# Image attention of a Flamingo kernel: scores per head pair, once with queries and once with keys on the partitions

## The reference

```python
l = layer_norm(layernorm(x), ln2_g, ln2_b)          # 4 batches x 512 rows x 128
c = layer_norm(ctx_1024, ln1_g, ln1_b)              # 4 x 154 x 128
q = l @ Wq                                          # 16 heads of 64
k, v = split(concat([c, l], axis=1) @ Wkv, 2)       # 666 keys and values a batch
w = softmax((q * 64 ** -0.25) @ (k * 64 ** -0.25).T)   # 512 x 666 for each batch and head
x = x + tanh(g_xattn[0]) * (w @ v) @ Wo
```

## Time and profile before

| | us |
|---|---|
| median of 3 runs | 2148.45 (2147.19 to 2157.12) |
| profiled execution, whole | 2145.17 |
| its span, first to last instruction | 2143.4 |
| busy in the span: PE, DVE, ACT, POOL | 1784.1, 1257.3, 969.9, 216.6 |
| image attention, first projection (L588) to last update of x (L710) | 17.8 to 795.6 |

### The profile page before, as it was taken

The page is one execution under the profiler, slowest core; times in us unless marked ns, Lnnn a source line. Parts: engine busy times, 40 slices in busy tenths (PEclk is TensorE's granted clock), DMA queues, the critical chain, the costliest instruction groups (busy, mean ns, idle before and its releaser), DMA issues.

```text
span 2143.4 us, 31509 instructions
## 1 busy us (share of the span) xinstructions
PE 1784.1 (83%) x11792; PEld 1060.9 (49%) x11792; DVE 1257.3 (59%) x2971; ACT 969.9 (45%) x2067; POOL 216.6 (10%) x263
## 2 busy tenths in 40 slices
PE   4899999999999987998615878995985886579997
PEld 2465655665665556776404544552443333324444
DVE  4766566656656644776496665655457455644333
ACT  3677667756756744996101624554211442201111
POOL 1100111111100000000000233300001301200000
PEclk9999999999999997999655879997997687779998
DMA  6000000000000010001000000000000000000000
GB/s 240 10 18 14 20 14 14 20 14 14 20 14 14 14 47 1 2 2 75 0 0 0 1 8 5 1 2 1 1 1 1 1 1 0 1 0 1 6 5 10
DMA packets 14584, 32.83 MB, mean 15 GB/s; under 512 B 3593, under 2 KB 9057, under 8 KB 13537
## 3 DMA queue, kind: packets, MB, share of 16 engines
q1 hardware_dynamic: 14433, 30.81, 4.6%
HBM read 18.84 MB, written 1.05 MB: 9 GB/s over the span
## 4 chain that ended last, share of the span: by engine, by line
PE 68%; DVE 22%; ACT 5%; issue 4%; POOL 2%; DMA 0%; ACTq 0%; DVEq 0%; POOLq 0%
PE banks L449 12%; PE banks L642 7%; PE banks L629 7%; PE banks L618 5%; PE banks L1589 3%; PE banks L2205 3%; PE banks L2201 3%; DVE work L668 3%; DVE xn L395 2%; DVE work L720 2%; PE banks L1572 2%; PE banks L573 1%; PE banks L2253 1%; PE banks L424 1%; PE banks L1498 1%
## 5 line engine op out<-in xcount | busy, mean ns | idle before, releaser
L749 ACT ACTIVATE work<-banks,work 128x666 f32<-128x666 f32 x256 | 209.1, 817 | 235.0 <-DVE work L668 205.5
L668 DVE TENSOR_REDUCE work<-banks 128x1 f32<-128x666 f32 x256 | 217.0, 848 | 84.8 <-PE banks L618 76.3
L642 PE MATMUL banks<-work 128*64 128x256 f32 (+1 forms) x1536 | 221.4, 395 | 13.8 <-ACT work L764 12.7
L629 PE MATMUL banks<-const,work 128*128 128x128 f32 (+1 forms) x1536 | 220.6, 280 | 6.3 <-ACT work L764 5.9
L449 PE MATMUL banks<-work,weights_b 128*128 128x512 bf16 x864 | 201.0, 389 | 13.1 <-DVE work L1913 5.2
L629 PEld LDWEIGHTS banks<-const,work 128*128 128x128 f32 (+1 forms) x1536 | 154.9, 134 | 80.3 <-issue 70.9
L618 PE MATMUL banks<-work 128*128 128x512 bf16 (+1 forms) x1024 | 188.3, 306 | 3.6 <-issue 3.6
L686 DVE COPY work<-banks 128x256 f32<-128x256 f32 x256 | 107.8, 421 | 84.8 <-PE banks L629 81.7
L618 PEld LDWEIGHTS banks<-work 128*128 128x128 bf16 x1024 | 97.9, 98 | 111.5 <-issue 41.6
L764 ACT ACTIVATE work<-banks 128x512 f32<-128x512 f32 x256 | 151.0, 590 | 2.1 <-PE banks L629 2.0
L424 PE MATMUL banks<-const,xn 128*128 128x128 f32 x176 | 39.3, 364 | 131.7 <-DVE xn L395 80.7
(11 more groups left out here) (344 smaller groups left out, 3130.2 us busy)
## 6 DMA issues: line engine op xcount, KB each, us to landing
work<-work SPq DMA_DIRECT2D x64, 166.5 KB, 2.7
weights_b<-in_weights SPq DMA_DIRECT2D x1, 4116.0 KB, 23.2
weights_b<-in_weights SPq DMA_DIRECT2D x1, 2824.0 KB, 9.3
weights_a<-in_weights SPq DMA_DIRECT2D x1, 2056.0 KB, 8.5
weights_a<-in_weights SPq DMA_DIRECT2D x1, 2050.0 KB, 9.5
rows<-in_rows SPq DMA_DIRECT2D x1, 1496.0 KB, 12.6
weights_c<-in_weights SPq DMA_DIRECT2D x1, 1288.0 KB, 26.3
weights_b<-in_weights SPq DMA_DIRECT2D x1, 1027.5 KB, 12.7
```

The costliest lines, as they stand in the source:

```text
L629: m = pe.transpose(ps[0:rows, c:c + P], prob[:, t * P:t * P + rows], self.eye)
L642: m = pe.matmul(self.out_bank[64 * h:64 * h + 64, 0:2 * P], self.v[n % 3][0:rows, t, 64 * h:64 * h + 64], self.probs_t[u % 2][0:rows, h, t ...
L668: ve.tensor_reduce(self.neg_max[i % 4], self.slot[i % 2][:, 0:KEYS0], AX_X, ALU.max, negate=True).then_inc(self.mark("max"))
L749: ac.activation(self.probs[i % 4], self.slot[i % 2][:, 0:KEYS0], ACT.Exp, bias=self.neg_max[i % 4], accum_out=self.sums[u % 2][:, 2 * j + ...
```

## The change

One image attention is replaced by another; the rest of the kernel stays. The work goes by pairs of heads n = 0 to 31. Scores are now made twice:

- with queries on the partitions, for the maxima alone (item "score", four a pair, both heads each): high half of q against bf16 keys, then the cross terms with the low halves. For the 512 image keys these are two matmuls that use 64 rows of the array each (L689, L690). VectorE takes both maxima ("max");
- with keys on the partitions (item "term", six a pair, the last with 26 keys): high part (L621), cross terms on 64 rows for each head (L624), and minus the maximum, which is turned by matmul ("lifted", L605), copied by ScalarE ("shifted") and added with ones over 32 rows for each head (L627). ScalarE then takes the exponential ("exp") straight into the operand of the values (L645; L643 for the 26). No probabilities are transposed, and none are copied.

The sums over keys are added by GpSimd over the terms ("sum"), and over the partitions by a matmul with ones ("total", L651); VectorE inverts 128 x 512 of them ("invert") and multiplies ("mix"). The two DMAs a pair now copy the high half of q. What is issued when is a table of times in pairs: a pair's projections are made during the pair before, its maxima in its own slot, its terms in the next, its total in the one after. All engines walk the sorted table.

```diff
-    def image_scores_pe(self, pe, i):
-        for a, z in ((0, SEQ), (SEQ, KEYS0)):
-            for part in (0, 1):
-                m = pe.matmul(slot[:, a:z], lhs, k[:, h, part, a:z], start=part == 0, stop=part == 1)
...
-    def image_turn_pe(self, pe, i):
-                m = pe.transpose(ps[0:rows, c:c + P], prob[:, t * P:t * P + rows], self.eye)
...
+    def image_items(self):
+
+        out = []
+        for n in range(GROUPS0):
+            first = n - 1 if n else -0.9
+            for at, what in ((0.02, "q"), (0.05, "q_high"), (0.14, "q_low"), (0.30, "k"), (0.33, "k_high"), (0.45, "k_low"),
+                             (0.60, "kc"), (0.63, "kc_high"), (0.76, "kc_low"), (0.78, "v"), (0.82, "v_keep")):
+                out.append((first + at, what, n, 0))
+            for i in range(QT):
+                out += [(n + 0.1 + 0.25 * i, "score", n, i), (n + 0.11 + 0.25 * i, "max", n, i)]
+            out += [(n + 0.98, "negate", n, 0), (n + 1.12, "lifted", n, 0), (n + 1.13, "shifted", n, 0)]
+            at = lambda i: n + 1.2 + 0.075 * i
+            for t in range(KT0):
+                out += [(at(2 * t), "term", n, t), (at(2 * t) + 0.001, "exp", n, t), (at(2 * t) + 0.002, "sum", n, t)]
+                out.append((at(2 * t + 3 if t < KT0 - 1 else 2 * t + 2), "weigh", n, t))
+            out.append((n + 2.17, "keep", n, 0))
+            out.append((n + 2.28, "total", n, 0))
+            out += [(n + 2.33 + 0.12 * j, "invert", n, j) for j in (0, 1)]
+            out += [(n + 2.36 + 0.12 * j, "mix", n, j) for j in (0, 1)]
+        for b in range(BATCH):
+            late = PAIRS * b + PAIRS + 1
+            for t, at in enumerate((0.8, 1.17, 1.8, 2.17)):
+                out += [(late + at, "bring", b, t), (late + at + 0.08, "add", b, t)]
...
+            elif what == "lifted":
+                bank = self.bank(pe, 7, "shifted", n)
+                if n == 0:
+                    pe.wait_ge(*self.at("dma_const_b", 16))
+                pe.wait_ge(*self.at("negated", n))
+                for t in range(QT):
+                    m = pe.matmul(bank[0:96, t * P:(t + 1) * P], self.neg_parts[n % 2][:, t, :], self.cb["eye_b"], start=True, stop=True)
+                m.then_inc(self.mark("lifted", n))
+            elif what == "term":
+                q_low, k, shifts = self.q_low[n % 3], self.k[n % 3], self.shifts[n % 2]
+                if i == 0:
+                    pe.wait_ge(*self.at("shifted", n))
+                    pe.wait_ge(*self.at("kc_low", n, 1))
+                rest = i == KT0 - 1
+                keys = slice(i * P, i * P + (WIDE if rest else P))
+                if rest:
+                    self.bank(pe, 3, "exp", n, i, 0)
+                    out = [self.bank_of(3)[0:WIDE, :], self.bank_of(3)[WIDE:2 * WIDE, :]]
+                else:
+                    out = [self.bank(pe, 3 + h, "exp", n, i, h) for h in (0, 1)]
+                width = WIDE if rest else P
+                for h in (0, 1):
+                    pe.matmul(out[h], k[:, h, keys], self.q_high[n % 3][:, h, :], start=True, stop=False)
+                for h in (0, 1):
+                    half = slice(D0 * h, D0 * (h + 1))
+                    pe.matmul(out[h], k[half, h, keys], q_low[half, :], start=False, stop=False)
+                for h in (0, 1):
+                    rows = slice(D0 * h, D0 * h + WIDE)
+                    m = pe.matmul(out[h], ones[rows, 0:width], shifts[rows, :], start=False, stop=True)
+                    if not rest:
+                        m.then_inc(self.mark("term", n, i, h))
+                if rest:
+                    m.then_inc(self.mark("term", n, i, 0))
+            elif what == "weigh":
+                if i == 0:
+                    self.bank(pe, 5, "out_kept", n)
+                    pe.wait_ge(*self.at("v_kept", n))
+                    pe.wait_ge(*self.at("vc_kept", n))
+                rest = i == KT0 - 1
+                pe.wait_ge(*self.at("exp", n, i, 0 if rest else 1))
+                for h in (0, 1):
+                    out = self.bank_of(5)[D0 * h:D0 * (h + 1), :]
+                    if rest:
+                        rows = slice(WIDE * h, WIDE * h + CTX_REST)
+                        m = pe.matmul(out, self.v_rest[n % 3][rows, :], self.image_prob(n, i, 0)[rows, :], start=False, stop=True)
+                    else:
+                        m = pe.matmul(out, self.v[n % 3][:, i, D0 * h:D0 * (h + 1)], self.image_prob(n, i, h), start=i == 0, stop=False)
+                m.then_inc(self.mark("weighed", n, i))
+            elif what == "total":
+                bank = self.bank(pe, 6, "inverted", n, 1)
+                pe.wait_ge(*self.at("summed", n, KT0 - 1))
+                for h in (0, 1):
+                    m = pe.matmul(bank[D0 * h:D0 * (h + 1), :], self.c["ones_f"], self.sums[n % 2][h], start=True, stop=True)
+                m.then_inc(self.mark("total", n))
...
+    def image_scores_pe(self, pe, n, i):
+
+        q_high, q_low, k = self.q_high[n % 3], self.q_low[n % 3], self.k[n % 3]
+        cols = slice(i * P, (i + 1) * P)
+        if i == 0:
+            for h in (0, 1):
+                pe.wait_ge(*self.at(f"dma_query{n % 2}{h}", 16 * (n // 2 + 1)))
+            pe.wait_ge(*self.at("q_low", n, 1))
+            pe.wait_ge(*self.at("kc_low", n, 1))
+            pe.wait_ge(*self.at("vc_kept", n))
+        main, rest = slice(0, SEQ), slice(SEQ, KEYS0)
+        first = self.bank(pe, 0, "max", n, i, 0)
+        pe.matmul(first, q_high[:, 0, cols], k[:, 0, main], start=True, stop=False)
+        shared = self.bank(pe, 1, "max", n, i, 1)
+        second = self.bank(pe, 2, "max", n, i, 1)
+        rests = [shared[:, 0:CTX], shared[:, BANK - CTX:BANK]]
+        pe.matmul(rests[0], q_high[:, 0, cols], k[:, 0, rest], start=True, stop=False, skip_group_check=True)
+        pe.matmul(rests[1], q_high[:, 1, cols], k[:, 1, rest], start=False, stop=False, skip_group_check=True)
+        pe.matmul(second, q_high[:, 1, cols], k[:, 1, main], start=True, stop=False)
+        own = slice(0, D0), slice(D0, P)
+        for h in (0, 1):
+            pe.matmul(rests[h], q_low[:, cols], self.k_rest[n % 3][:, h, :], start=False, stop=True, skip_group_check=True)
+        pe.matmul(first, q_low[own[0], cols], k[own[0], 0, main], start=False, stop=True)
+        pe.matmul(second, q_low[own[1], cols], k[own[1], 1, main], start=False, stop=True).then_inc(self.mark("score", n, i))
...
+            elif what == "max":
+                if i == 0 and n >= 2:
+                    ve.wait_ge(*self.at("negated", n - 2))
+                ve.wait_ge(*self.at("score", n, i))
+                for h in (0, 1):
+                    src = self.psum[:, 0:KEYS0] if h == 0 else self.psum[:, 3 * BANK - KEYS0:3 * BANK]
+                    ve.tensor_reduce(self.neg_max[n % 2][:, i, h:h + 1], src, AX_X, ALU.max, negate=True).then_inc(self.mark("max", n, i, h))
+            elif what == "negate":
+                ve.wait_ge(*self.at("max", n, QT - 1, 1))
+                ve.wait_ge(*(self.at("lifted", n - 2) if n >= 2 else self.at("clear_parts", 1)))
+                most = self.neg_max[n % 2]
+                parts = self.neg_parts[n % 2].rearrange("p t (h n) -> p t h n", n=WIDE)[:, :, 0:3:2, 0:2]
+                ve.wait_ge(*self.own("ve", ve.tensor_copy(parts[:, :, :, 0], most)))
+                ve.tensor_tensor(parts[:, :, :, 1], most, parts[:, :, :, 0], ALU.subtract).then_inc(self.mark("negated", n))
+            elif what == "invert":
+                ve.wait_ge(*self.at("total", n))
+                if n:
+                    ve.wait_ge(*self.at("mixed", n - 1, i))
+                cols = slice(i * HALF, (i + 1) * HALF)
+                ve.reciprocal(self.inverse[:, cols], self.bank_of(6)[:, cols]).then_inc(self.mark("inverted", n, i))
+            elif what == "mix":
+                cols = slice(i * HALF, (i + 1) * HALF)
+                mixed = self.mixed[n % MIXED][:, cols]
+                ve.wait_ge(*self.at("out_kept", n))
+                ve.wait_ge(*self.at("inverted", n, i))
+                ve.tensor_tensor(mixed, mixed, self.inverse[:, cols], ALU.mult).then_inc(self.mark("mixed", n, i))
...
+            elif what == "shifted":
+                ac.wait_ge(*self.at("lifted", n))
+                ac.activation(self.shifts[n % 2][0:96, :], self.bank_of(7)[0:96, :], ACT.Copy).then_inc(self.mark("shifted", n))
+            elif what == "exp":
+                for h in (0, 1) if i < KT0 - 1 else (0,):
+                    old = self.image_old_prob(n, i, h)
+                    if old:
+                        ac.wait_ge(*self.at("weighed", *old))
+                        ac.wait_ge(*self.at("summed", old[0], max(old[1], 1)))
+                    ac.wait_ge(*self.at("term", n, i, h))
+                    rows = slice(0, P if i < KT0 - 1 else 2 * WIDE)
+                    ac.activation(self.image_prob(n, i, h)[rows, :], self.bank_of(3 + h)[rows, :], ACT.Exp).then_inc(self.mark("exp", n, i, h))
...
```

(40 more changed lines are left out.)

426 lines of the change are left out of this document (164 added, 262 removed).

## The result

| | before | after |
|---|---|---|
| median, us | 2150.06 (2147.19 to 2157.12, 4 runs) | 2260.82 (2253.06 to 2264.64, 4 runs) |
| ratio | | 1.0505, 95% interval 1.0467 to 1.0544 |
| image attention ends at, us in the span | 795.6 | 905.8 |
| the rest of the span behind it, us | 1347.8 | 1352.5 |
| distance from one pair to the next, steady, us | 21.83 | 24.33 |

A forecast was written before the change was run, and what follows sets the result against it. TensorE's queue was taken to bound image attention: 17.8 + streams 602 + changes 131 + waits 70 + start and end 14 = 835 us against 795.6, +39, so 2186 us for the kernel; 8-in-10 range 2115 to 2270.

The forecast's parts named there:

- The streams of the row pieces: TensorE's matmuls on part of the rows run beside each other; all streams 18.8 us a pair, 602 us.
- The rival of serial pieces: TensorE's row pieces run behind each other: 109 us more, kernel at 2295 us; chance 0.10.
- The price of a change: TensorE, changed shape of the used array: 37 a pair at 0.10 or 0.16 us, 131 us in all.
- The rival of free changes of rows: Changes of rows alone cost TensorE nothing: 64 us go, kernel at 2122 us; chance 0.17.
- The steady waits: TensorE waits 1.0 before the first term, 0.4 between terms 1 and 2, 0.8 before the total: 2.2 a pair, 70 us.
- The 0.4 between terms 1 and 2: TensorE waits 0.4 us for two exponentials (1.55 with hops), with only one product of the values (1.1) between.
- The others: VectorE 15, ScalarE 12.3, GpSimd 11.6 us a pair, all beside TensorE's 25; inverse taken as 1.8 us.
- GpSimd's rival: GpSimd's adds and weight splitting become the bound: some 2 us a pair more, kernel at 2245 us; chance 0.07.
- The count of a pair: TensorE's steady pair with Wo: 25.1 us from one L605 to the next.
- the 14 us for start and end: TensorE idle at first maxima and last pair together, 14 us (bounds 5 to 30); first scores about 10 us sooner.
- the sum built on it: Image attention ends at 17.8 + 602 + 131 + 70 + 14 = 835 us against 795.6, +39 us.
- The clock: TensorE's granted clock stays at 1.00, the 2.4 GHz level, throughout the image attention.

The follow-up runs named there:

- e3: Changed kernel with the ones for subtracting the maximum over 64 rows a head instead of 32; 2237.49 us, ratio 1.0414 to the kernel before.
- e4: As e3, and the two 64-row matmuls of each score come first instead of last; 2238.09 us, ratio 1.04 to the kernel before.
- e10: Changed kernel with the low half of q made before the maxima and the turned maxima and their copy before the score; 2183.04 us, ratio 1.0136.
- e2: Changed kernel with the turned maxima and their copy placed before the first score of the slot; 2282.8 us, ratio 1.0626 to the kernel before.
- e5: Changed kernel with GpSimd's adds of terms 2 to 4 covering 4 of 512 columns, sums incomplete; 2246.36 us, ratio 1.0437 to the kernel before.
- e7: Changed kernel with the weight loads of stages 1 to 4 issued behind the first two pairs' query DMAs; 2254.7 us, ratio 1.0496.
- e9: As e8, with the turn of the next batch's columns after term 5 instead of before the product ahead of it; 2139.04 us, ratio 0.9928.
- e8: Changed kernel with the edits of e10, e4 and e7 together; 2150.49 us, ratio 0.9993 to the kernel before.

## Why the prediction was right in direction and off by 75 us

**The streams of the row pieces: right.** L689 and L690 start 0.01 us apart, and the row pieces of the terms run beside each other too: a pair L624 takes 0.32, a pair L627 0.32, with the change in it, where 0.43 and a change would be one behind the other. The rival of serial pieces is out. The sentence of the Trainium skill ("TensorE: Matmul & The Clock Gate", Part 3) on distinct row groups holds here.

**The price of a change: right.** The forecast took 0.10, for rows alone as well. One change read directly is 0.10 (e3); as distance, with the longer wait in it, 0.087 (e3) and 0.093 (e4) are left. The rival of free changes of rows is out. The rule of the Trainium skill ("TensorEngine Tiling (Array Packing)", Key Properties), that a change of tiling mode drains TensorE, agrees with these numbers.

**The steady waits: right in kind, smaller.** 0.69 and 0.81 for 1.0 and 0.8. The 0.4 between terms 1 and 2 was forecast from an order that only 4 of the 32 pairs have (n = 3 to 6): there it is (0.34 us of waiting, and 24.72 for the pair at the full clock). Score 1 and term 1 both have the table time n + 1.35, and the rounding of the sum decides which comes first; in the other pairs the score comes behind term 1 and fills the wait. 1.6 a pair for 2.2 (e10). What I had not seen is that the first two share one stretch of VectorE (e2).

**The others: right.** L744 took 1754 ns for 1.8, L870 1275 for 1159. Neither VectorE nor GpSimd is the bound. GpSimd's rival fell with e5.

**The count of a pair: right, in part by luck.** 25.1 less 0.9 for Wo is 24.2, and 24.33 was measured. But the waits were 0.6 shorter than forecast and the rest 0.7 longer: without both waits the pair takes 22.71 (e10), where the forecast has 24.2 - 2.2 = 22.0. A part of that may stand in these rows: the projections of the context took 0.93 where 0.59 stood, and L605 (start 400.30, with 0.69 idle before L621 at 401.41) 0.42 where 0.2 stood.

```profile
412.06 0.54 PE L586 MATMUL banks<-ctxn_t,weights_a 128*128 128x160 f32 x2
...
412.99 0.60 PE L621 MATMUL banks<-work 128*128 128x512 bf16 x2
```

**The step that failed is the 14 us for start and end, and the sum built on it.** The stage is 888.0 us. Less 32 x 24.33 = 778.6 and 28.8 for Wo, 80.6 are left where the sum had 14. These 66.6 and 0.13 x 32 = 4.2 of the pair are the 70.8 us between the forecast end of 835 and 905.8. (The rest of the 75 is behind the stage.) What is in the 80.6:

- The start. I had the first scores 10 us sooner; they came at 36.17, 0.7 later than before (35.44). I counted the keys' copy as gone, but not that its successor, the copy of q, had to land behind weights (e7).
- The pairs with Wo. L713 now stands behind two maxima, and Wo's bank waits for it: 17.0 us in six waits. The distances with Wo in them exceed the steady one by 46.9 us in sum, before by 34.3.
- The first pairs. The table puts the turn of the columns of batches 1 to 3 (L426) into the second to fourth pair, and there it waits 4.1, 4.1 and 1.3 us for L724 (moving it gave 11 us, e9). Not all of this is new: the turn before (L424) waited 6.8 us in its three times for L686. The first eight distances exceed the steady one by 20.1 us, before by 12.4. The forecast priced the new order only in a steady pair; the items that come in a few pairs alone stood in the same order.
- The clock. I wrote 1.00 throughout. It is 0.96 over the stage: 47.8 us at the 1.2 GHz level between 55 us and the last pair, before none. More of them came where the waits were longer (e2: 92.2 us), fewer where waits were gone (e10: 17.1, e9: 6.8). The wait alone doesn't decide it. The group of Wo at 294.29, behind a wait of 2.83 us, ran at the full clock, and so did the next; the one at 323.86, behind the same wait, took 3.44 us, and the granted level had fallen at 323.42:

```profile
294.29 2.02 PE L659 MATMUL banks<-weights_a,work 128*128 128x128 f32 x16 [2.83 <-DVE work L713]
311.19 2.05 PE L659 MATMUL banks<-weights_a,work 128*128 128x128 f32 x16
323.86 3.44 PE L659 MATMUL banks<-weights_a,work 128*128 128x128 f32 x16 [2.83 <-DVE work L713]
```

  Sixteen passes of Wo took 3.75 us at the lower level and 2.02 at the full one, so as an estimate the 47.8 us cost at most 24.
- The last pair: the terms came at 2.6 us each as forecast, but the total, inverse, product and four groups of Wo (two of them at 3.75 us, two at 2.02) had been put into the same 14.

And the sum was held against something that isn't its like. I counted 22.2 us a pair for the kernel before (with Wo) and saw that its stage holds more than the count; I took that for tails. By the same arithmetic the stage before, 777.8 us, leaves 777.8 - 32 x 21.83 - 28.8 = 50.4 us outside its steady pairs. The forecast set a bare count of the new stage, with 14, against a measured old one, with 50. "The pair goes from 23.2 to 25.1" has the same fault: 23.2 is neither the count with Wo (22.2) nor the stage shared out (777.8 / 32 = 24.3), and the steady pair was 21.83 and became 24.33. Had the 50.4 been carried over and nothing else changed, the sum would have been 17.8 + 32 x 24.2 + 28.8 + 50.4 = 871.4, which is 2221 us: 36.4 of the 70.8, half of the miss. Another 30.2 are what the new order added at start, first pairs, Wo, end and in the clock, and 4.2 the pair. The forecast's own two counts say the same more simply: 803 with changes and waits (and without the 14) against 711 is 92 us more, not 39, and 111 were measured.

The cause is settled for the changes and the waits of the pair (e3, e4, e10); for most of the rest e8 and e9 support it: they take waits, some of the changes and the DMA away, and 118.5 us are gone. That isn't a split of the 110: some of what they take away (the turn's waits) had its like before. Open is how much the clock alone costs; no run changed the clock without changing a wait.

## What to carry to other kernels

Set a count of the new against the same count of the old, and carry over what the old trace holds beyond its count; the difference of the counts is the forecast, not count minus measurement. When an order is written as a table, walk it also where the rare items stand (every eighth pair, first, last), for a wait priced only in the steady part is underpriced, and give no two items of one queue the same time. Two waits of one engine under the same stretch of another are one wait: remove both or neither.

## What the runs showed of the hardware that was not expected

**A cast or a product of VectorE on SBUF stands still until GpSimd's running operation ends.** L737 casts 8 elements a partition from fp32 to bf16, SBUF to SBUF, in 0.17 to 0.19 us. In 22 of its 31 rows between 60 and 880 us one of GpSimd's fp32 adds was running when it began, and in each of these it ended 0.04 or 0.05 us behind the end of that add, however long that took. GpSimd's and VectorE's timelines of the changed kernel, in two places: the adds end at 397.05 and the cast at 397.09; the copy L894 ends at 437.81 and the product L750, with two inputs in SBUF, at 438.09 (alone it takes 0.43, as at 430.79).

```profile
391.93 5.12 POOL L870 TENSOR_TENSOR work<-work 128x512 f32<-128x512 f32 x4
397.20 2.59 POOL L866 TENSOR_TENSOR work<-work 26x512 f32<-26x512 f32 x2
...
436.77 1.04 POOL L894 COPY weights_b<-split 128x1024 bf16<-128x1024 bf16 x1
```

```profile
395.89 1.20 DVE L737 CAST work<-work 128x8 bf16<-128x8 f32 x1
...
430.79 0.43 DVE L750 TENSOR_TENSOR work<-work 128x256 f32<-128x256 f32 x1
436.93 1.16 DVE L750 TENSOR_TENSOR work<-work 128x256 f32<-128x256 f32 x1
```

With the short adds of e5 the cast finds none to wait for. From 30 to 900 us, first the changed kernel, then e5 (count, busy, mean ns):

```profile
L737 DVE CAST work<-work 128x8 bf16<-128x8 f32 x32 | 25.2, 788 | 0.8
L397 DVE TENSOR_SCALAR xn<-x,norm_room 128x128 f32<-128x128 f32 x12 | 9.8, 878 | 0.0
L750 DVE TENSOR_TENSOR work<-work 128x256 f32<-128x256 f32 x64 | 45.5, 711 | 4.6 <-DVE work L744 0.5
```

```profile
L737 DVE CAST work<-work 128x8 bf16<-128x8 f32 x32 | 5.9, 184 | 0.8
L397 DVE TENSOR_SCALAR xn<-x,norm_room 128x128 f32<-128x128 f32 x12 | 4.8, 462 | 0.0
L750 DVE TENSOR_TENSOR work<-work 128x256 f32<-128x256 f32 x64 | 38.4, 600 | 4.6 <-DVE work L744 0.5
```

The forecast had weighed a rule of the Trainium skill on this and said that only the products could meet GpSimd; it overlooked the casts and L397, which read one tile. The Trainium skill ("SBUF — State Buffer", section "SBUF: two separate sides") calls the shared pair of ports an exclusive lock that the first comer holds for its whole instruction; the rows above agree, with GpSimd as the first comer. In a steady pair it costs VectorE 1.0 us for the cast (1.20 less 0.18), and 0.7 for the second product (1.16 less 0.43), all beside TensorE's work. The product's part is not the new adds' doing: in the steady pairs it meets the copy L894 of the experts' weights, as above, and it keeps its 1.16 us in e5. Whether the adds' part is in e5's 4.0 us between the marks, no run separates.

**A change of rows costs about as much as a change of columns**: 0.10 us from 64 to 32 rows (e3) against 0.105 from full to column halves, both out of a bf16 piece, while two pieces in distinct rows start 0.01 us apart.
